# Mamba-2 block on 8 cores: the causal convolution split in two blocks, the first emitted between the halves of the input projection

## What is computed

```python
h = rmsnorm(xn, norm_w)
zxbcdt = einsum('bld,ed->ble', h, in_proj_w)           # 1024 -> 2048 + 2304 + 32
z, xBC, dt = split(zxbcdt, [2048, 2048 + 2304])
conv = causal depthwise convolution of xBC over time, 4 taps, 2304 channels
xBC = silu(conv + conv_b)
x, B, C = split(xBC, [2048, 2048 + 128])
dt = softplus(dt + dt_bias)
# state scan over time: h = h * exp(dt*A) + dt*B*x ; y = C*h + D*x
# y = rmsnorm(y * silu(z), ssm_norm_w) @ out_proj_w ; then the two MLPs
```

## Time and profile before

| what | us |
|---|---|
| median of the two runs shown (4452.36 and 4570.03) | 4511.19 |
| the profiled execution | 4451.24 |
| its span, slowest core (core 0) | 4449.6 |
| spans of the eight cores | 4413.2 to 4449.6 |

### The profile page before, as it was taken

The page is one execution under the profiler, slowest core; times in us unless marked ns, Lnnn a source line. Parts: engine busy times, 40 slices in busy tenths (PEclk is TensorE's granted clock), DMA queues, the critical chain, the costliest instruction groups (busy, mean ns, idle before and its releaser), DMA issues.

```text
span 4449.6 us, 36396 instructions; the slowest of 8 cores (4413.2 to 4449.6 us)
## 1 busy us (share of the span) xinstructions
PE 2302.5 (52%) x9681; PEld 1018.2 (23%) x9681; DVE 1807.9 (41%) x3925; ACT 558.3 (13%) x1011; POOL 156.2 (4%) x160
## 2 busy tenths in 40 slices
PE   0536603437870143434343433677777746878877
PEld 0212201113330011111111111233333312333333
DVE  3532496652219656565656561122222201222222
ACT  3000021000122212121212120111111100000000
POOL 0110000000010000000000000000000000000000
PEclk9998855558985555555555556778888867889988
DMA  5562000011120311111111119100000074111111
GB/s 165 187 163 62 19 0 1 1 28 34 39 75 0 86 44 57 45 55 47 54 48 53 48 43 157 29 19 20 19 24 24 15 118 103 35 34 44 39 34 36
DMA packets 94289, 234.09 MB, mean 53 GB/s; under 512 B 23984, under 2 KB 26832, under 8 KB 93456
## 3 DMA queue, kind: packets, MB, share of 16 engines
q0 software_dynamic: 40448, 106.44, 10.6%
q1 hardware_dynamic: 51344, 116.94, 8.6%
q10 hardware_dynamic: 2304, 8.39, 0.5%
HBM read 235.13 MB, written 51.66 MB: 64 GB/s over the span
## 4 chain that ended last, share of the span: by engine, by line
PE 43%; DVE 21%; issue 15%; DMA 13%; ACT 5%; DVEq 1%; another core or an unknown queue 1%; SPq 0%; ACTq 0%; POOL 0%; POOLq 0%
PE P L1068 4%; PE P L1231 4%; PE P L1235 4%; PE P L930 3%; PE P L420 3%; PE P L425 3%; PE P L1072 3%; DMA bcast<-lam_dram 3%; DMA wbuf<-w_in 3%; DVE Emt L845 2%; PE P L1271 2%; PE P L1110 2%; PE PS L1271 2%; PE P L645 2%; PE PS L1110 2%
## 5 line engine op out<-in xcount | busy, mean ns | idle before, releaser
L851 PE MATMUL P<-x_tok,Emt 128*128 128x64 bf16 x512 | 108.6, 212 | 293.3 <-DVE Emt L845 283.1
L549 DVE SCALAR_TENSOR_TENSOR B_acc<-xbc,c_convw,B_acc 128x2048 bf16<-128x2048 bf16 x108 | 245.3, 2344 | 0.0
L1253 DVE TENSOR_TENSOR F_h<-F_h,P 128x1024 bf16<-128x1024 bf16 x48 | 58.6, 1221 | 386.9 <-ACT F_h L1247 386.9
L836 ACT ACTIVATE Est<-Est 128x128 f32<-128x128 f32 x512 | 155.7, 309 | 434.1 <-DVE Est L830 432.6
L1090 DVE TENSOR_TENSOR E_h<-E_h,P 128x1024 bf16<-128x1024 bf16 (+1 forms) x48 | 53.3, 1110 | 384.4 <-ACT E_h L1084 384.4
L1231 PE MATMUL P<-wg,F_xf 128*128 128x512 bf16 x384 | 149.5, 389 | 86.2 <-DMA wg<-w_g 44.0
L332 PE MATMUL P<-c_identf,A_n 128*128 128x128 f32 x256 | 90.5, 445 | 199.5 <-DVE A_n L320 167.7
L1068 PE MATMUL P<-wg,E_hnT 128*128 128x512 bf16 x384 | 147.6, 408 | 84.0 <-ACT E_h L1084 61.3
L845 DVE SCALAR_TENSOR_TENSOR Emt<-Est,dtk,Gm 128x128 bf16<-128x128 f32 x512 | 175.8, 346 | 9.1 <-PE P L851 6.5
L645 PE MATMUL P<-c_identf,dt 32*128 32x32 f32 x32 | 8.9, 278 | 321.1 <-issue 161.5
L830 DVE TENSOR_SCALAR Est<-bcast,lam_tok 128x128 f32<-128x128 f32 x512 | 152.5, 303 | 53.6 <-DMA bcast<-lam_dram 4.0
(11 more groups left out here) (198 smaller groups left out, 4305.4 us busy)
## 6 DMA issues: line engine op xcount, KB each, us to landing
bcast<-lam_dram SPq DMA_DIRECT2D x64, 512.0 KB
A_x<-x_own SPq DMA_DIRECT2D x32, 512.0 KB, 4.2
A_x<-x_pre SPq DMA_DIRECT2D x32, 512.0 KB, 4.3
wd<-w_d POOLq DMA_DIRECT2D x2, 5376.0 KB, 60.9
wg<-w_g POOLq DMA_DIRECT2D x5, 2048.0 KB, 44.1
wu<-w_u POOLq DMA_DIRECT2D x5, 2048.0 KB, 48.8
xn_dram<-A_n POOLq DMA_DIRECT2D x16, 512.0 KB, 4.8
xfh<-xfp_dram SPq DMA_DIRECT2D x4, 2048.0 KB, 14.2
```

The costliest lines, as they stand in the source:

```text
L549: e.scalar_tensor_tensor(a[:, :], xbc[:, ec * CW + k:ec * CW + k + T], self.c["convw"][:, ec * 4 + k:ec * 4 + k + 1], a[:, :], ALU.mult, A ...
L836: t_ee[h] = self.op("scalar", lambda e, q3=q3: e.activation(est[q3][:, :], est[q3][:, :], AF.Exp), wait=[("sq", gq + 1) if lastg else ("sv ...
```

## The change

The convolution is put in a function `emit_conv(lo, hi)` and called twice: for blocks 0 to 8 right after the first half of the weights has been used (before the second half's weights are loaded, in program order), and for blocks 9 to 17 where all of it stood before. The pads are handled in `emit_pads`, once for each call. `B_acc` moves up by 4096 bytes, so that it no longer shares bytes with `zst`, and the wait of the pads for the stores of z and for ACT goes. In place of the wait for all evictions stands one for the last eviction of the blocks in question. The arithmetic, the sizes and the count of the large instructions stay as they are.

```diff
         uid = 0
         t_wv = getattr(self, "t_wdone", None)
+        acc = [cv(f"B_acc{q}", OFF["R_C"] + 20480 + q * 4096, [128, T], BF16)
+               for q in range(3)]
+        t_conv = {}
+        t_silu = {}
+        self.op("vector", lambda e: e.memset(
+            bass.AP(xbc, 2051, [[NCC * CW, 128], [CW, NCC], [1, 1]]), 0.0),
+            inc=("sv", 1))
+
+        def emit_pads(lo, hi):
+            n = hi - lo
+            if pre:
+                pz = self.op("vector", lambda e, lo=lo, n=n: e.memset(
+                    bass.AP(xbc, lo * CW, [[NCC * CW, 128], [CW, n], [1, 3]]), 0.0),
+                    wait=[("sv", ev_ec[hi - 1])], inc=("sv", 1))
+                tp = self.op("vector", lambda e, lo=lo, n=n: e.tensor_copy(
+                    bass.AP(self.pads_sb, lo * 3, [[NCC * 3, 128], [3, n], [1, 3]]),
+                    bass.AP(xbc, lo * CW + 2048, [[NCC * CW, 128], [CW, n], [1, 3]])),
+                    wait=[("sv", ev_ec[hi - 1])], inc=("sv", 1))
+                self.t_pads = tp
+                return pz, tp
+            pz = self.op("vector", lambda e, lo=lo, n=n: e.tensor_copy(
+                bass.AP(xbc, lo * CW, [[NCC * CW, 128], [CW, n], [1, 3]]),
+                bass.AP(self.pads_sb, lo * 3, [[NCC * 3, 128], [3, n], [1, 3]])),
+                wait=[("sv", self.t_pads)], inc=("sv", 1))
+            return pz, None
+
+        def emit_conv(lo, hi):
+            pz, tp = emit_pads(lo, hi)
+            for g in range(lo, hi, 3):
+                grp = list(range(g, min(g + 3, hi)))
+                for step in range(4):
+                    for j, ec in enumerate(grp):
+                        a = acc[j]
+                        if step == 0:
+                            t_conv[ec] = self.op("vector", lambda e, ec=ec, a=a:
+                                e.tensor_scalar(
+                                    a[:, :], xbc[:, ec * CW:ec * CW + T],
+                                    self.c["convw"][:, ec * 4:ec * 4 + 1], None,
+                                    ALU.mult),
+                                wait=[("sv", pz), ("sv", ev_ec[ec]),
+                                      ("sa", t_silu.get(ec - 3))],
+                                inc=("sv", 1))
...
@@ -435,6 +493,8 @@
                         wait=[("st", mm), ("dr", t_r1)], inc=("sv", 1))
+                    if th == 1:
+                        ev_ec[ec] = t_ev[uid]
                     uid += 1
...
+            if halfw == 0 and b_stop != "mm":
+                emit_conv(0, 9)
         self.t_wdone = self.cnt["st"]
...
         if b_stop == "mm":
             return
-        t_evall = self.cnt["sv"]
...
-        else:
-            pz = self.op("vector", lambda e: e.tensor_copy(
-                bass.AP(xbc, 0, [[NCC * CW, 128], [CW, NCC], [1, 3]]),
-                bass.AP(self.pads_sb, 0, [[NCC * 3, 128], [3, NCC], [1, 3]])),
-                wait=[("sv", self.t_pads), ("sv", t_evall),
-                      ("dn0", self.cnt["dn0"]), ("dn1", self.cnt["dn1"]),
-                      ("sa", self.cnt["sa"])], inc=("sv", 1))
-
-        acc = [cv(f"B_acc{q}", OFF["R_C"] + 16384 + q * 4096, [128, T], BF16)
-               for q in range(3)]
-        t_conv = {}
-        t_silu = {}
-        for g in range(0, NCC, 3):
...
+        emit_conv(9, NCC)
         self.t_xbc = self.cnt["sa"]
```

More of the change, by code:

```diff
@@ L382, in phase_B @@
         t_mm = {}
+        ev_ec = {}
         uid = 0
         t_wv = getattr(self, "t_wdone", None)
+        acc = [cv(f"B_acc{q}", OFF["R_C"] + 20480 + q * 4096, [128, T], BF16)
[22 more added lines that the diff above has]
+            return pz, None
@@ new lines, in emit_conv @@
+        def emit_conv(lo, hi):
[14 more added lines that the diff above has]
+                                inc=("sv", 1))
+                        else:
+                            t_conv[ec] = self.op("vector", lambda e, ec=ec, a=a, k=step:
+                                e.scalar_tensor_tensor(
+                                    a[:, :], xbc[:, ec * CW + k:ec * CW + k + T],
+                                    self.c["convw"][:, ec * 4 + k:ec * 4 + k + 1],
+                                    a[:, :], ALU.mult, ALU.add),
+                                wait=[("sv", t_conv[ec])], inc=("sv", 1))
+                for j, ec in enumerate(grp):
+                    t_silu[ec] = self.op("scalar", lambda e, ec=ec, a=acc[j]:
+                        e.activation(
+                            xbc[:, ec * CW + 3:ec * CW + 3 + T], a[:, :], AF.Silu,
+                            bias=self.c["convb"][:, ec:ec + 1]),
+                        wait=[("sv", t_conv[ec])] +
+                             ([("sv", tp)] if pre else []),
+                        inc=("sa", 1))
```

## The result

The change made the kernel faster: median 4396.69 us of 11 runs, against 4515.37 us of 10 runs of the kernel before in the same session. Medians of all runs mix in executions in which one die ran at a lower clock; the comparisons leave these out, and give a ratio of 0.9856, 95% interval 0.9816 to 0.9896. On the 4451.24 us of the profiled execution before, that is 64 us less (46 to 82), and the forecast was 61.6. The profiled execution after took 4396.69 us.

A forecast was written before the change was run, and what follows sets the result against it. DVE and PE were taken to alternate in one chain, no engine above 52% busy. Hidden weight loads (24.3 pre, 15.4 own) plus a group beside z (21.9) sum to 61.6 us off 4451.2: 4390 us, range 4370 to 4440.

The forecast's parts named there:

- What bounds the kernel: Convolution, projection and z: no engine above 52% busy; DVE and PE alternate in one chain, stage by stage.
- The block's price: Convolution block of three groups on DVE: 69.6 us for the first of each half, 69.0 for the second.
- The sum: Whole kernel: 24.3 + 15.4 + 21.9 = 61.6 us off 4451.2, giving 4390; gain 1.4%, called under a measurable 2%.
- 24.3 (pre): Pre half: 23.7 us of weight-load wait hidden, plus about one Silu gap fewer against one more pad.
- 37.3 (own): Own half: 15.4 us from a hidden second weight load and 21.9 from a convolution group beside z.
- the middle: Convolution block between the projection's weight halves: hides the second weight load, gaining 24.3 us in pre, 15.4 in own.
- z: Own half's z stage: just one group of three hidden on DVE beside it, gaining 21.9 us.
- Where a group waits: Own half's z stage: after one group, DVE waits about 38 us for Silus queued behind ACT's z evictions.
- Starved loads: Rival: in the moved blocks DVE holds back POOL's DMA descriptors, loads land late, 10 us gain left, 4441; chance 0.07.
- Cold PE: Rival: after about 75 us idle before each second half, PE stays at 1.2 GHz, 4528 us; chance 0.02.
- Only the middle: Rival: the group beside z costs as much as it saves, total 4412 us; chance 0.06.
- the rivals: Alternatives for the whole kernel: starved loads 0.07, only the middle 0.06, cold PE 0.02; nothing moves, excluded.

The follow-up runs named there:

- alone-parts: Changed kernel with only the block between the weight halves kept: 4416.36 us, 0.9914; with only the convolution's freedom to start before z ends kept: 4431.12 us, 0.9950.
- The two timings: The changed kernel against the kernel before, timed in two comparisons: ratio 0.9856, then 0.9838.
- Late load: Changed kernel, POOL's load of the second half's weights held until the first group of three convolution blocks is through: 4379.37 us, one execution.
- late fast: Same held weight load, and each `scalar_tensor_tensor` of blocks 0 to 8 replaced by three fast `tensor_scalar`: 4405.2 us, one execution.
- z-alone kernel: Changed kernel without the block between weight halves; all six groups after z in program order, free to start before z ends: 4431.12 us, ratio 0.9950.
- the repeat: The unmodified changed kernel timed again against the kernel before: median 4385.84 us, ratio 0.9838 (0.9815 to 0.9861).
- Interleaving: Changed kernel with convolution instructions emitted singly between other units: own half's blocks 9 to 17 with z, 4337.77 us, 0.9735; all, in both projection halves, 4224.81 us, 0.9482.

## Why the prediction was right and where it was wrong

**What bounds the kernel** held: the same busy times, a shorter span.

**The block's price** held: 69.65 and 69.5 us against 69.6; PE stood still for 75.30 us ahead of the second half, against "about 73 to 75".

**The sum.** Forecast 24.3 (pre) + 37.3 (own) = 61.6 us. Measured on core 0: 23.6 + 34.8 = 58.4, and the alone-parts put 38 on the middle (forecast 39.7) and 22 on z (forecast 21.9). Of the 2.5 us missing in the own half, 2.0 lie between the start of L454's scaling and the end of the second scaling of z's weights: 171.5 us after, 169.5 before. DVE's two waits for z's weights are 1.8 of them (87.6 against 85.8). They were taken as fixed, and vary by some us from one execution to the next. The two timings, 64 and 72 us, lie above the 58; what they gain outside the two stretches wasn't forecast and isn't explained.

**Where a group waits** held: 38.45 us for the Silus, against "about 38".

**Starved loads** fell in the changed kernel itself: the scaling waits for no load, and on core 0 the two loads beside the block landed after 23.4 and 15.8 us, against 24.5 and 16.2 before. Late load and late fast show that the two engines do hold one another, by 0.3 to 0.4 us at an issue. **Cold PE** fell: after 75.30 us idle, PE ran its first matmuls at a granted clock of 0.50 (1.2 GHz) for 5.0 us, and then rose,

```profile
497.26 0.58 PE L478 MATMUL P<-xfh,wbuf 128*128 128x512 bf16 x1 [75.30 <-DVE wbuf L454]
...
502.28 0.43 PE L478 MATMUL P<-xfh,wbuf 128*128 128x512 bf16 x1
```

against 4.2 us after 28.97 us of pause and 5.1 after 48.96: no growth with the pause, and in the own half of the kernel before it took 5.1 us after only 20.69. (The 0.43 us of the later matmul is core 3's 0.81 clock again; on core 0 it is 0.38 us, 5.4 us after the first.) **Only the middle** fell with the z-alone kernel.

**The step that was wrong** is the last of the sum: "under the 2% or so that a measurement of this kernel can tell from no change". The gain did come out within 2%, where 0.93 had been put; wrong is that this was taken for no change that a measurement can tell. The first timing has an interval of 0.4% to either side, wholly below 1; the repeat 0.23%, the kernels with single parts 0.15%, and even 22 us (0.9950, at most 0.9964) is told from none. The 2% was read from no row; all that was at hand were two times, 4452.36 and 4570.03 us, which differ by 2.6%, and such a spread isn't the width of a comparison's interval. A working that forecasts 61.6 us with bounds of 45 to 80 should say "faster", and give "no change" only what the rivals take.

**The change itself** is less than a third of what was to be had. The block in the middle hides 24 and 15 us of load wait, but PE stands still for 75 us meanwhile; the two engines still take turns. Interleaving showed that the same instructions fit in the gaps: 231 us instead of 64 to 72.

## What to carry to other kernels

When two engines take turns, moving a whole block of one of them into a wait gains only the wait; look at whether single instructions fit between the other engine's units, and compare the recorded start-to-start distances, not the durations, with the pace that must hold. What can hide behind a stage is set by the in-order queue of the next consumer: count the buffers that are freed only behind that stage's work. Before calling a gain too small to tell, find the interval that a comparison of this kernel gives; the spread of two times doesn't give it.

## What the hardware showed that was not expected

DVE instructions one behind the other start earlier than the recorded end of the one before: 1.23 us evictions and 2.34 us instructions alternate at 3.45 us. DVE and POOL hold each other: a DVE instruction of 0.75 us took 1.04 beside an issue, and an issue of 0.89 us took 1.33 beside fast DVE work. And in the profiled execution of the changed kernel cores 2 and 3 were granted 0.81 of the clock for a stretch in which cores 0, 1 and the other die had 1.00, at a cost of 0.75 us a unit (4.20 for 3.45) while it lasted.
